# Turning the residual rows back in three tiles instead of four, and writing the feed-forward loop out

## The reference

```
x = x + attention(layernorm(x), ctx, seg)      # low-rank latent attention, 16 heads, 9-key window
x = x + ffn(layernorm(x))                      # silu(x Wg^T * sg) * (x Wu^T * su), then Wd^T * sd; inner 1408
```

## Time and profile before

| | us |
|---|---|
| median of three runs | 772.26 |
| the profiled execution, whole | 765.55 |
| its span, first to last instruction | 763.8 |
| TensorE matmuls busy | 714.3 (94%) |
| VectorE busy | 461.5 (60%) |
| ScalarE busy | 395.8 (52%) |
| GpSimd busy | 212.5 (28%) |

### The profile page before, as it was taken

How to read it: one execution, slowest core, us unless ns; L and a number is a source line. 1 busy time by engine, 2 the same in 40 slices (tenths; PEclk the granted TensorE clock), 3 DMA queues, 4 the chain that set the end, 5 groups by cost and what they waited for, 6 DMA issues and landing times.

```text
span 763.8 us, 17758 instructions
## 1 busy us (share of the span) xinstructions
PE 714.3 (94%) x6970; PEld 665.9 (87%) x6970; DVE 461.5 (60%) x947; ACT 395.8 (52%) x885; POOL 212.5 (28%) x334
## 2 busy tenths in 40 slices
PE   4989789999999999999999999989889999999997
PEld 4878659779987899779987998779879999999997
DVE  2989845765477446755467446768794544536342
ACT  5868635684357635674358535678552332323230
POOL 1656752614044311604054222530330000000000
PEclk9999989999999999999999999999999999999999
DMA  8999974054313442044313433048101212021111
GB/s 281 268 353 297 309 204 110 13 129 89 89 47 105 88 82 77 11 125 91 93 36 106 85 80 83 3 162 328 44 27 35 71 36 62 7 69 34 35 52 35
DMA packets 46357, 81.19 MB, mean 106 GB/s; under 512 B 5482, under 2 KB 30106, under 8 KB 46282
## 3 DMA queue, kind: packets, MB, share of 16 engines
q1 hardware_dynamic: 40796, 53.67, 26.5%
q0 software_dynamic: 5488, 26.50, 10.1%
HBM read 57.26 MB, written 11.28 MB: 90 GB/s over the span
## 4 chain that ended last, share of the span: by engine, by line
PE 72%; DVE 13%; ACT 6%; DMA 6%; issue 3%; POOL 0%; SPq 0%; DVEq 0%; ACTq 0%; POOLq 0%
PE ps L1446 14%; PE ps L1136 12%; PE ps L999 10%; PE ps L1481 8%; PE ps L1141 6%; PE ps L1074 4%; PE ps L189 3%; PE ps L1047 3%; DMA head_w<-head_w_dram 2%; ACT q_lat L1179 2%; PE ps L1009 2%; PE ps L1038 2%; DVE ffn_lo L831 2%; PE ps L1063 1%; PE ps L527 1%
## 5 line engine op out<-in xcount | busy, mean ns | idle before, releaser
L1288 DVE TENSOR_TENSOR o_parts<-q_lat,o_parts 128x320 fp32r<-128x320 f32 x80 | 68.0, 869 | 67.4 <-ACT o_parts L1187 67.4
L1136 PE MATMUL ps<-o_parts,wvo_hi 128*128 128x320 f32 x320 | 96.7, 312 | 1.8 <-ACT o_parts L1187 1.8
L1136 PE MATMUL ps<-o_parts,wvo_lo 128*128 128x320 f32 x320 | 95.8, 310 | 0.0
L1187 ACT ACTIVATE o_parts<-q_lat 128x320 fp32r<-128x320 f32 x80 | 63.7, 820 | 46.7 <-PE ps L1136 45.6
L1521 ACT ACTIVATE silu<-ps,ffn_scale 128x320 f32<-128x320 f32 x55 | 29.0, 527 | 94.6 <-PE ps L1446 94.3
L935 POOL TENSOR_TENSOR rot_c<-gathered,cosq 128x192 f32<-128x192 f32 x40 | 25.6, 641 | 163.8 <-PE ps L1009 145.4
L1136 PEld LDWEIGHTS ps<-o_parts,wvo_hi 128*128 128x128 f32 x320 | 60.6, 190 | 2.3 <-ACT o_parts L1187 2.0
L1571 DVE SCALAR_TENSOR_TENSOR hidden<-ps,ffn_scale,silu 128x320 f32<-128x320 f32 x55 | 30.2, 549 | 53.2 <-ACT silu L1521 47.1
L1136 PEld LDWEIGHTS ps<-o_parts,wvo_lo 128*128 128x128 f32 x320 | 60.5, 189 | 0.3
L1141 PE MATMUL ps<-o_parts,wvo_hi 128*128 128x320 f32 x320 | 60.4, 310 | 0.0
L527 PE MATMUL ps<-wkv,ctx_hi 128*128 128x384 f32 x192 | 54.9, 398 | 5.2 <-ACT ctx_hi L389 5.2
(11 more groups left out here) (170 smaller groups left out, 1847.6 us busy)
## 6 DMA issues: line engine op xcount, KB each, us to landing
ctx_raw<-ctxT_dram SPq DMA_DIRECT2D x16, 722.0 KB, 7.9
gathered<-key_rows SPq DMA_DIRECT2D x240, 47.2 KB
head_w<-head_w_dram SPq DMA_DIRECT2D x16, 576.0 KB, 5.2
ffn_raw<-ffn_w_dram POOLq DMA_DIRECT2D x11, 768.0 KB, 12.8
kv_table<-tab POOLq DMA_DIRECT2D x16, 288.0 KB, 6.3
rows<-x_dram SPq DMA_DIRECT2D x5, 640.0 KB, 5.1
residual<-x_dram SPq DMA_DIRECT2D x20, 160.0 KB, 2.5
x_rows<-residual SPq DMA_DIRECT2D x20, 160.0 KB, 2.0
```

Of the source, the lines that this page charges most:

```text
L1136: last = pe.matmul(ps[:, 4 + m, 0:TB], w[wt][:, h, cols], o_hi[h % RING], start=(h == 0 and n == 0), stop=False, skip_group_check=True)
L1187: act.activation(o_hi[h % RING], q_lat[:, h % 2, :, h // 2], ACT.Copy).then_inc(oh_ok, 1)
L1288: dve.tensor_tensor(o_lo[h % RING], q_lat[:, h % 2, :, h // 2], o_hi[h % RING].bitcast(F32), ALU.subtract).then_inc(ol_ok, 1)
```

## The change

Residual tiles have 128, 128 and 64 tokens (`RT`, `RTILES` = 3). A turn back has 12 transposes instead of 16, 3 adds instead of 4, and 3 loads and 3 stores instead of 4 and 4. Tiles 0 and 2 use buffer 0, tile 1 uses buffer 1. The adds in attention stand behind o = 5, 7 and 13. In the FFN tiles 0 and 1 stay behind c = 0 and tile 2 is behind c = 3. All FFN blocks are written out on every engine. LayerNorm keeps its tiles of 80.

```diff
+RT = 128
+RTILES = (TB + RT - 1) // RT
...
-        sums = [sb(f"residual{i}", [LT, D]) for i in range(2)]
+        sums = [sb(f"residual{i}", [RT, D]) for i in range(2)]
...
     def rest(self, sp, b):
-        for t in range(0, NLT, 2):
-            self.store(sp, b, t)
-            self.store(sp, b, t + 1)
-            if t + 2 < NLT:
-                self.load(sp, b, t + 2)
-                self.load(sp, b, t + 3)
+        self.store(sp, b, 0)
+        self.store(sp, b, 1)
+        self.load(sp, b, 2)
+        self.store(sp, b, 2)
...
-        dve.tensor_tensor(self.rows[i][:, :], bank, self.rows[i][:, :], ALU.add).then_inc(self.summed, 1)
+        dve.tensor_tensor(self.rows[i][0:self.size(t), :], bank[0:self.size(t), :], self.rows[i][0:self.size(t), :],
+                          ALU.add).then_inc(self.summed, 1)
...
-        for t in range(NLT):
+        for t in range(RTILES):
+            n = res.size(t)
             for c in range(KC):
-                last = pe.transpose(ps[0:LT, 4 + t, c * P:(c + 1) * P], oT[:, c, t * LT:(t + 1) * LT],
-                                    ident[:, :])
+                last = pe.transpose(ps[0:n, 4 + t, c * P:(c + 1) * P], oT[:, c, t * RT:t * RT + n], ident[:, :])
...
-                    pe.wait_ge(res.summed, c4(b - 1, o - 19))
+                    pe.wait_ge(res.summed, Count(RTILES)(b - 1, min(o - 19, RTILES)))
...
-        adds, stats = (5, 7, 13, 17), (3, 9, 15, 21)
+        adds, stats = (5, 7, 13), (3, 9, 15, 21)
...
-                    for t in ((0, 1) if c == 0 else (2, 3)):
+                    for t in ((0, 1) if c == 0 else (2,)):
                         turn_back(b - 1, t)
...
-        with pe.Fori(1, BLOCKS - 1) as b:
-            body(b, False, False, some_low)
-        body(BLOCKS - 1, False, True, some_low)
+        for b in range(1, BLOCKS):
+            body(b, False, b == BLOCKS - 1, some_low)
...
-                for t in range(2, NLT):
-                    dve.wait_ge(y_mm, c4(b, t + 1))
-                    dve.tensor_tensor(rows[:, t, :], ps[0:LT, 6 + t % 2, :], rows[:, t, :],
-                                      ALU.add).then_inc(res.summed, 1)
+                n = res.size(2)
+                dve.wait_ge(tail_in, 16)
+                dve.wait_ge(y_mm, c3(b, RTILES))
+                dve.tensor_tensor(rows[0:n, 2, :], ps[0:n, 6, :], rows[0:n, 2, :], ALU.add).then_inc(res.summed, 1)
```

More of the change, by code:

```diff
@@ L667, in __init__, with size, uses @@
         self.stored = [sem(f"{tag}_out{i}") for i in range(2)]
+    @staticmethod
+    def size(t):
+        return min(RT, TB - t * RT)
+    @staticmethod
+    def uses(i, blocks, t=0):
+        return 16 * (blocks * len(range(i, RTILES, 2)) + len(range(i, t, 2)))
     def _tile(self, ap, b, t):
-        return ap[bass.ds(b * TB + t * LT, LT), :]
+        return ap[bass.ds(b * TB + t * RT, self.size(t)), :]
     def load(self, sp, b, t, fresh=False):
@@ L1382, in _ @@
         sp.dma_start(scale[:, :], a["ffn_scale"]).then_inc(s_in, 16)
[L1383 to L1387, removed]
+        attn_res.wait_stored(sp, 2)
+        unrolled(sp, body)
+        tail = slice((BLOCKS - 1) * TB + 2 * RT, TOK)
+        n = res.size(2)
         sp.wait_ge(ln.turned, NLT * BLOCKS)
-        for t in range(2, NLT):
-            sp.dma_start(rows[:, t, :], tail[0][t * LT:(t + 1) * LT, :]).then_inc(tail_in, 16)
+        sp.dma_start(rows[0:n, 2, :], x1[tail, :]).then_inc(tail_in, 16)
         for t in range(2):
             res.store(sp, BLOCKS - 1, t)
[L1393 to L1398, removed]
+        sp.wait_ge(res.summed, RTILES * BLOCKS)
+        sp.dma_start(a["out"][tail, :], rows[0:n, 2, :]).then_inc(tail_out, 16)
+        for i, s in enumerate(res.stored):
+            sp.wait_ge(s, res.uses(i, BLOCKS - 1, 2))
+        sp.wait_ge(tail_out, 16)
     @block.gpsimd
@@ L1562, in add_back @@
         def add_back(b, t):
-            res.add(dve, b, t, y_mm, ps[0:LT, 6 + t % 2, :])
+            res.add(dve, b, t, y_mm, ps[:, 6 + t % 2, :])
         def body(b, first, last):
@@ L1578, in body @@
                 if first and c < 2:
-                    attn_add_back(dve, BLOCKS - 1, 2 * c)
-                    attn_add_back(dve, BLOCKS - 1, 2 * c + 1)
+                    for t in ((0, 1) if c == 0 else (2,)):
+                        attn_add_back(dve, BLOCKS - 1, t)
                 if not first and c in (0, 3):
-                    for t in ((0, 1) if c == 0 else (2, 3)):
+                    for t in ((0, 1) if c == 0 else (2,)):
                         add_back(b - 1, t)
@@ L1606, in _ @@
         low_flag_out()
-        body(0, True, False)
-        with dve.Fori(1, BLOCKS - 1) as b:
-            body(b, False, False)
-        body(BLOCKS - 1, False, True)
+        unrolled(dve, body)
 def constants():
```

43 lines of the change are left out of this document (18 added, 25 removed).

## The result

The changed kernel took 765.88 us (median of 8 runs, 763.03 to 769.02), the kernel before 770.32 in the same rounds (8 runs, 765.88 to 772.77). The ratio is 0.9946, with a 95% interval of 0.9921 to 0.9972: 4.2 us faster, between 2.2 and 6.1. The forecast was a gain of 4.05 us and a time of 768.2, range 766.4 to 771.3.

A forecast was written before the change was run, and what follows sets the result against it. TensorE, busy 94% of the span, was taken as the bound, except in the last attention block and FFN block 0. Gains 1.31 + 1.74 - 0.2 + 0.6 + 0.6 + 0 = 4.05 us; 772.26 became 768.2 us, range 766.4 to 771.3.

The forecast's parts named there:

- The level: Whole kernel: compared runs' median stays 6.7 us above the profiled execution, so 772.26 less 4.05 gives 768.2 us.
- Term 1: Turn backs: four fewer transposes at 0.109 us save 0.44 us each; 1.31 in attention blocks 1-3, 1.74 in FFN blocks 1-4.
- Rival (b): Transposes: weight loads set their distance in proportion to columns, so their saving falls to 0; 771.3 us, chance 0.05.
- Term 2: Last attention block: its turn back saves nothing and add 2 comes 0.35 us later; a loss of 0.2 us.
- rival (c): Last attention block keeps its 0.44 us, its load not late; FFN block 0 gains 1.2; 766.8 us, chance 0.08.
- The wait of product o = 19 grows to 0.8: Last attention block: sign of being right, TensorE's wait at this product growing from 0.45 to 0.8 us.
- Term 3: FFN block 0: one add fewer puts VectorE 0.67 us earlier, so the block ends 0.6 us earlier.
- Rival (a): Last attention block and FFN block 0: larger stores delay dependent loads and eat the gain; up to 771.1 us, chance 0.17.
- Term 4: Kernel's end: the last add starts at 759.80 as tile 2's does now and one add goes; 0.6 us gained.
- Term 5: FFN blocks: writing them out instead of looping changes nothing, 0 us, bounds -0.3 and +0.3.
- The sum: Whole kernel: 1.31 + 1.74 - 0.2 + 0.6 + 0.6 + 0 = 4.05 us gained.

The follow-up runs named there:

- padded: The changed kernel with tile 2's four transposes done twice in every turn back, 16 again; 767.48 us, ratio 1.0004 to the kernel before.
- written_out_only: The kernel before, tiles of 80 kept, with only the FFN blocks written out; 766.97 us, ratio 0.9999 to the kernel before.
- halves: The changed kernel with new tiles in one stage only, 80-token tiles in the other: attention 766.06 us, ratio 0.9985; FFN 765.18 us, ratio 0.9961.
- spare: The changed kernel with the last attention tile's residual rows loaded early into their own buffer; 769.2 us, ratio 1.0016 to the kernel before.

## Why the prediction was right in its gain and wrong in its time

**The level: the step that failed.** "The runs that are compared have their median 6.7 us above the profiled one. [...] so 772.26 - 4.05 = 768.2 us." Three runs were taken for the level of the kernel before. It read 770.32 with 8 runs, and 767.75, 767.99, 767.78 and 767.99 in the four later jobs. Of the 2.3 us between 768.2 and the measured 765.88, 1.9 are this level and 0.4 is the gain, 4.4 between the medians instead of 4.05. The 6.7 us were no property of the kernel but the distance of one execution from those three: the second profiled execution of the same kernel lay 4.1 us above its median (771.68 against 767.58), not below. Executions differ in stages that the change does not touch; the part before the first query product lasted 113.8 to 117.3 us from trace to trace. The range had 0.4 us for "the scatter of a median (the runs before lie up to 1.75 us from theirs)"; that spread was of three runs and should have been a term of the size of the gain.

**Term 1, right.** 1.31 us for 12, blocks of 41.46 to 41.50, and padded shows that the transposes are what counts. Rival (b) falls: loads that set the distance by their columns would have left the 16 x 80 and the 8 x 128 + 4 x 64 columns equal, 1280 in both, and the traces have 1.75 and 1.31. No run shows the distance of transposes in proportion to their columns. The load records themselves grow far less than the columns: 111 ns for 64 in the changed kernel, 118 for 80 and 140 for 128.

**Term 2, wrong in sign.** "A shorter turn back brings TensorE to this wait 0.44 us earlier and it waits 0.44 longer: this turn back saves nothing." The wait was treated as fixed to the block. It belongs to SP's copies, whose end moves: in both traces of the changed kernel the rows of the last block were in time, its stretch fell from 16.95 to 15.09, and the late rows stood in blocks 2 and 3. For block 4 that is no chance of one execution: the load started 2.2 to 3.0 us behind the first query product in all four traces with attention tiles of 80 and rows in their old place, and 0.3 to 2.2 us ahead of it in all nine with three tiles and 12 transposes; in padded it was 1.2 behind. Why the copies end earlier there and later in blocks 2 and 3 was not tried. Over all four stretches the mean of three traces is 63.8 with 16 transposes and 61.7 with 12 (the one other trace with tiles of 80 and late rows has 63.2, the six others with 12 transposes 60.8 to 62.3), a gain of 2.1 where I had 1.31 - 0.2 = 1.1. That is rival (c) for this block, though not by a faster load: by an earlier one. "The wait of product o = 19 grows to 0.8": there is none in the trace.

**Term 3, near in size, wrong in its mechanism.** 0.6 forecast, 0.39 measured (51.70 to 51.31). The forecast came from VectorE: one add fewer, while "the 0.44 of TensorE is hidden under its own wait of 1.60". The traces have it the other way round. GpSimd's operation and VectorE's low part behind the last add, before and changed:

```profile
550.60 3.47 POOL L831 TENSOR_TENSOR ffn_lo<-ffn_raw,hi_front 128x1536 fp32r<-128x1536 f32 x1 [0.83 <-ACT hi_front L826]
553.57 2.12 DVE L831 TENSOR_TENSOR ffn_lo<-ffn_raw,hi_front 128x1536 fp32r<-128x1536 f32 x1
```

```profile
552.33 3.47 POOL L833 TENSOR_TENSOR ffn_lo<-ffn_raw,hi_front 128x1536 fp32r<-128x1536 f32 x1 [0.40 <-ACT hi_front L828]
554.89 2.53 DVE L833 TENSOR_TENSOR ffn_lo<-ffn_raw,hi_front 128x1536 fp32r<-128x1536 f32 x1
```

Counted from the block's start (538.75 and 540.90), the low part starts 0.83 us earlier, but it ends 1.62 us behind GpSimd's operation in both. So the add that is gone bought nothing. The 0.42 us that the low part ends earlier, and the block with it, is how much earlier GpSimd's operation ran. It waits for ScalarE's high part, and ScalarE's silu ahead of that waited for TensorE 0.85 us before and 0.41 after: these are the four transposes. Padded has the three adds with 16 transposes; there GpSimd's operation starts as late as before, 11.86 us into the block (11.85 before, 11.43 changed), and the low part again ends 1.62 us behind it. TensorE's wait of 1.60 shrank to 1.20 where I had 1.0, and its next one grew from 0.51 to 0.92. The block is 51.7 in three of the five traces with attention tiles of 80 and 51.3 in all four with three tiles and no other edit near it. The other two, the second of the kernel before and written_out_only, have 53.25, with the granted clock down to 0.50 near the block's end. Rival (a) falls: neither special place lost anything to its DMAs.

**Term 4, a little large.** 0.6 forecast, 0.4 to 0.5 in the traces.

**Term 5, right.** 0.9999 (0.9979 to 1.0019) for the writing out alone.

**The sum.** By place 2.1 + 0.4 + 1.76 + 0.45 = 4.7 us. Timed: 4.2, 3.2 and 3.1 us in three measurements of the tiles, and 1.2 + 3.0 by halves. The first interval holds 4.7, the other two end at 4.5 and 4.3. A difference of 0.5 to 1.5 us may be left; the median granted clock of the runs was 0.9865 and 0.986 for the tiles against 0.988 before in that job, and within a kernel 0.001 went with 0.2 to 0.7 us, so 0.3 to 1.4 us in all could come from it. In the jobs of the halves the clocks were alike. It stays open.

Not foreseen at all was the largest cost near the edit, 6 us in FFN block 0 from the overlap with GpSimd. The rows for it were on record: a low part of 2.04 us in the chain where the usual one is 1.74. I read it as VectorE having too much to do.

## What to carry to other kernels

The transposes of this kernel are counted, not measured by their stationary columns (0.109 us each with 64, 80 and 128): make fewer of them by filling the stationary side. Forecast a ratio, and give the absolute level of three runs an uncertainty of its own. Before an engine's wait is priced or removed, look at the durations of one operation across the stage: where they differed here, another engine was in it, an earlier start bought nothing, and in spare it made things worse.

## What the runs showed of the hardware that I had not expected

**TensorE's granted clock falls for a few microseconds at a time.** Windows of the changed kernel at the start of the attention stage's last output product (the last three numbers are the granted clock, the DMA share and GB/s):

```profile
506.00:509.00 3.00, 1.44 (x20) 1.10 (x18) 0.89 (x2) 2.69 (x7) 0.45 (x1) 1.00 0.40 91
509.00:512.00 3.00, 1.94 (x7) 1.94 (x8) 1.96 (x3) 2.97 (x5) 3.00 (x7) 0.50 1.09 301
512.00:515.00 3.00, 3.00 (x13) 3.00 (x12) 1.61 (x3) 0.87 (x2) 2.47 (x5) 0.50 1.00 408
515.00:518.00 3.00, 3.00 (x19) 3.00 (x19) 1.30 (x2) 1.23 (x2) 0.00 (x0) 0.86 1.02 418
518.00:521.00 3.00, 3.00 (x23) 3.00 (x22) 1.84 (x2) 2.35 (x4) 0.00 (x0) 1.00 1.02 420
```

TensorE was busy for 1.44 of 3 us, then its granted clock stood at 0.50, and at 1.00 again from 518 on; full windows have 23 matmuls, the slow one 13. Such dips also come inside dense work: a block's attention steps take 38.18 us at a granted clock of 1.00 in most traces, and 39.8 at 0.96 or 41.3 at 0.92 in some, in kernels of every kind.

**Pauses of TensorE in one execution only.** The first trace of the changed kernel has four like this one, at 156, 241, 327 and 412 us; the second has none.

```profile
156.29 0.85 PE L1048 MATMUL ps<-key_latT,q_lat 128*56 128x63 f32 x22 [0.24 <-issue]
```

They are in steps that the change does not touch and go with the 38.7 to 38.9 us of those blocks. The profile shows nothing that TensorE waited for in them ("issue"); what made them was not tried.
